# The last group of tails moved two to three turns earlier, and the first 22 tiles placed from six units' counts

## What is computed

```
h = concat(patches @ W + b with a class token and position embedding, txt)
h = h + attention(layernorm(h))                 # 12 heads of 16, rotary, causal
x = layernorm(h)                                # 8768 tokens, all samples together
pc = softmax(x @ Wsc + bsc); e = argmax(pc)     # "common" expert, 4 of them
dropped = rank of a token in its expert by -pmax >= capacity (2192)
u = argmax(softmax(x @ Wsu + bsu))              # "unique" expert, 4 of them
out = h + ffn_common[e](x) + dropped * ffn_unique[u](x)     # ffn: 192 -> 768 -> 192, gelu
```

## Time and profile before

| what | value |
|---|---|
| median of 3 runs | 1402.95 us (1399.99, 1402.95, 1414.35) |
| the profiled execution | 1410.49 us, its span 1408.7 us |
| mean granted TensorE clock in it | 0.941 |
| PE busy | 1227.0 us, 87% of the span |
| DVE, POOL, ACT busy | 905.9, 623.0, 557.8 us |
| data moved | 177.93 MB, mean 126 GB/s |

### The profile page before, as it was taken

How to read it: one execution, slowest core, us unless ns; L and a number is a source line. 1 busy time by engine, 2 the same in 40 slices (tenths; PEclk the granted TensorE clock), 3 DMA queues, 4 the chain that set the end, 5 groups by cost and what they waited for, 6 DMA issues and landing times.

```text
span 1408.7 us, 33272 instructions
## 1 busy us (share of the span) xinstructions
PE 1227.0 (87%) x12722; PEld 1041.6 (74%) x12722; DVE 905.9 (64%) x2063; ACT 557.8 (40%) x959; POOL 623.0 (44%) x990
## 2 busy tenths in 40 slices
PE   5889999999999999999999997648997778989983
PEld 4667777777777777777777766538896677989983
DVE  5676776786786786787787785467875333445431
ACT  1234334334334334334334343224453333545540
POOL 4133333334544444444444434426326364655654
PEclk9899999999999999999999997659998897999997
DMA  6001211212322322322322312477766364777740
GB/s 206 21 20 45 73 39 47 77 59 83 127 63 84 125 66 83 122 69 83 122 69 82 102 51 84 148 288 255 268 237 192 122 210 156 257 246 262 235 151 25
DMA packets 84368, 177.93 MB, mean 126 GB/s; under 512 B 16446, under 2 KB 57701, under 8 KB 84208
## 3 DMA queue, kind: packets, MB, share of 16 engines
q1 hardware_dynamic: 70544, 146.93, 32.2%
q0 software_dynamic: 13664, 28.84, 5.7%
HBM read 129.15 MB, written 50.38 MB: 127 GB/s over the span
## 4 chain that ended last, share of the span: by engine, by line
PE 43%; DVE 21%; issue 14%; POOL 10%; ACT 6%; another core or an unknown queue 2%; DMA 2%; SPq 1%; DVEq 0%; POOLq 0%; ACTq 0%
PE h_ps L1655 10%; PE y_ps L1666 10%; DVE capped L971 4%; ACT PT L739 3%; PE gen L502 3%; PE round_banks L582 3%; POOL sorted_d L226 3%; DVE xn L987 3%; POOL PT L853 3%; PE round_banks L555 2%; PE gen L544 2%; DVE nm L975 2%; PE gen L511 2%; DVE nm L973 2%
## 5 line engine op out<-in xcount | busy, mean ns | idle before, releaser
L739 ACT ACTIVATE PT<-round_banks 128x1752 f32<-128x1752 f32 x96 | 156.6, 1631 | 176.7 <-PE round_banks L582 176.7
L853 POOL TENSOR_SCALAR_AFFINE_SELECT PT<-PT 128x512 f32<-128x512 f32 x192 | 117.7, 637 | 212.5 <-ACT PT L739 212.0
L1745 ACT ACTIVATE Gl<-h_ps,W 128x256 f32<-128x256 f32 x264 | 117.3, 474 | 233.6 <-PE h_ps L1655 141.4
L1655 PE MATMUL h_ps<-XH,Wh 128*128 128x256 f32 x528 | 155.6, 310 | 51.2 <-issue 32.3
L1666 PE MATMUL y_ps<-W,Gl 128*128 128x192 f32 x1056 | 186.6, 331 | 0.9 <-issue 0.9
L1666 PEld LDWEIGHTS y_ps<-W,Gl 128*128 128x128 f32 x1056 | 176.5, 194 | 1.1 <-issue 1.1
L1655 PEld LDWEIGHTS h_ps<-XH,Wh 128*128 128x128 f32 x528 | 107.5, 204 | 57.7 <-issue 44.4
L502 PE MATMUL gen<-w_emb,xT 128*128 128x192 f32 (+1 forms) x768 | 142.5, 337 | 7.6 <-DMA ident<-in_ident_dram 7.6
L1655 PE MATMUL h_ps<-XH,Wl 128*128 128x256 f32 x528 | 145.5, 295 | 0.0
L1814 DVE TENSOR_TENSOR Wl<-W,Wh 128x768 fp32r<-128x768 f32 x88 | 84.2, 957 | 88.0 <-ACT Wh L1725 58.9
L1554 POOL DMA_INDIRECT out_dram<-Y,sid x76 | 81.3, 1070 | 134.3 <-DVE Y L1838 112.6
(11 more groups left out here) (273 smaller groups left out, 2467.0 us busy)
## 6 DMA issues: line engine op xcount, KB each, us to landing
W<-in_experts_dram SPq DMA_DIRECT2D x44, 771.0 KB
W<-in_experts_dram SPq DMA_DIRECT2D x44, 672.0 KB
xT<-in_xT_dram SPq DMA_DIRECT2D x32, 591.0 KB
X<-sorted_d SPq DMA_DIRECT2D x35, 450.0 KB
stage<-rows_d SPq DMA_DIRECT2D x64, 224.0 KB
rows_d<-xn SPq DMA_DIRECT2D x32, 256.0 KB
rows_d<-h SPq DMA_DIRECT2D x32, 192.0 KB
out_dram<-h SPq DMA_DIRECT2D x32, 192.0 KB
```

The lines of the kernel that those rows point to most:

```text
L739: act.activation(PT[(JG * b + j) % 2][:], R[:, :, 0:438], ACT.Exp, scale=SCALE).then_inc(exps, 1)
L853: pool.affine_select(x[:, :, at:at + P], x[:, :, at:at + P], [[0, GH], [1, P]], ALU.is_ge, 0.0, base=0, channel_multiplier=-1)
L1655: mm = pe.matmul(h_ps[f % 3][:, 0:ROWS], w[t.par][:, cols], x, start=(k == 0), stop=(k == len(products) - 1))
L1745: act.activation(Gl[t.par][:, f, :], h_ps[f % 3][:, 0:ROWS], ACT.Gelu, bias=W[t.i][:, B1O + f:B1O + f + 1]).then_inc(g_ready, 1)
```

## The change

In the last group (7) the tail steps of lags 8 to 12 move from turns 36, 37, 38, 39, 40 to turns 35, 36, 36, 37, 37 (`HURRIED`). The table `FINAL` says the order of banks in turns 35 and 36. On PE `rank` of unit 6 goes to the front of turn 36, the transposes `X2t` behind those of sample 31, `RTt` behind `RT`. On DVE `position` of unit 6 goes ahead of the copies of logits in turn 36, and `soften` waits for both copies. `early_tiles` goes from turn 37 to turn 33 and uses the counts of six units; EARLY is 22 in place of 26. The first row load waits for the scatters of units 0 to 5. `load_both` depends on EARLY, so it is issued at tiles 24 to 26 in place of 28 to 30.

```diff
--- before.py
+++ after.py
@@ -51,7 +51,7 @@
 RC = DX + D
 RW = RC + 2
 GROUP = 3
-EARLY = -(-(N - N // NG - NX * (ROWS - 1)) // ROWS)
+EARLY = -(-(N - 2 * (N // NG) - NX * (ROWS - 1)) // ROWS)
 NOWHERE = 2.0 ** 14
 AWAY = 2.0 ** 17
 KTH = CT
@@ -68,11 +68,19 @@
 TURNS = 4 * (NG - 1) + 12 + 1
 
 
+LAST = 4 * (NG - 1)
+HURRIED = {"8": LAST + 7, "9": LAST + 8, "10": LAST + 8, "11": LAST + 9, "12": LAST + 9}
+FINAL = {LAST + 7: [use for use in STEADY if use[0] not in ("ATt", "WO", "WOt")] + [("ATt", "8"), ("WO", 4), ("WOt", "8")],
+         LAST + 8: [("RK", "12"), ("X2", 5), ("X2t", "9"), ("RT", 5), ("RTt", "10")]}
+
+
 def item(lag, t):
 
     if isinstance(lag, str):
+        if HURRIED.get(lag) == t:
+            return NG - 1
         g, rest = divmod(t - int(lag), 4)
-        return g if rest == 0 and 0 <= g < NG else None
+        return g if rest == 0 and 0 <= g < NG - (lag in HURRIED) else None
     return t - lag if 0 <= t - lag < B else None
 
 
@@ -80,7 +88,7 @@
 
     table = {}
     for t in range(TURNS):
-        for use, lag in uses:
+        for use, lag in FINAL.get(t, uses) if uses is STEADY else uses:
             if item(lag, t) is not None:
                 table[use, item(lag, t)] = len(table)
     return table
@@ -96,6 +104,7 @@
     def __init__(self, t):
         self.t = t
         self.new, self.pre, self.mid, self.at, self.fin, self.end = (item(k, t) for k in range(6))
+        self.hurried = t >= LAST + 7
         self.tail = {k: item(str(k), t) for k in (0, 1, 7, 8, 9, 10, 11, 12)}
 
 
@@ -612,6 +621,8 @@
             for t in map(Turn, range(TURNS)):
                 if t.t == 2:
                     pe.wait_ge(later_in, 16 * len(later))
+                if t.hurried and t.tail[12] is not None:
+                    rank(t.tail[12])
                 if t.mid is not None:
                     for c in range(3):
                         have(f"KQ{c}", t.mid)
@@ -653,6 +664,9 @@
                 if t.end is not None:
                     pe.wait_ge(xn2_ready, t.end + 1)
                     turn_tokens("X2", t.end, xn2[t.end % 2], 2)
+                if t.hurried and t.tail[9] is not None:
+                    pe.wait_ge(xn2t_ready, t.tail[9] + 1)
+                    turn_tokens("X2t", t.tail[9], xn2t, 1)
                 if t.pre is not None:
                     project("V1", t.pre, xnT, w_qkv, 1, slice(2 * D, 3 * D))
                 if t.at is not None:
@@ -666,10 +680,10 @@
                         pe.wait_ge(consts_set, n_set)
                     pe.wait_ge(xnt_ready, t.tail[0] + 1)
                     turn_tokens("XTt", t.tail[0], xnt, 1)
-                if t.tail[8] is not None:
+                if t.tail[8] is not None and not t.hurried:
                     have("UTt", t.tail[8])
                     turn_tokens("ATt", t.tail[8], attt, 1)
-                if t.tail[10] is not None:
+                if t.tail[10] is not None and not t.hurried:
                     have("X2t", t.tail[10])
                     route("RTt", t.tail[10], x2tT, 1)
                 if t.tail[7] is not None:
@@ -684,12 +698,18 @@
                 if t.end is not None:
                     have("X2", t.end)
                     route("RT", t.end, x2T, 2)
-                if t.tail[12] is not None:
+                if t.hurried and t.tail[8] is not None:
+                    have("UTt", t.tail[8])
+                    turn_tokens("ATt", t.tail[8], attt, 1)
+                if t.hurried and t.tail[10] is not None:
+                    have("X2t", t.tail[10])
+                    route("RTt", t.tail[10], x2tT, 1)
+                if t.tail[12] is not None and not t.hurried:
                     rank(t.tail[12])
                 if t.tail[0] is not None:
                     have("XTt", t.tail[0])
                     project("QKt", t.tail[0], xntT, w_qkv, 0, slice(0, 2 * D))
-                if t.tail[9] is not None:
+                if t.tail[9] is not None and not t.hurried:
                     pe.wait_ge(xn2t_ready, t.tail[9] + 1)
                     turn_tokens("X2t", t.tail[9], xn2t, 1)
                 if t.pre is not None:
@@ -795,6 +815,9 @@
 
                         act.wait_ge(g_filled[bank("WO", t.fin - 1)], nth("WO", t.fin - 1))
                     copy_tokens("AT", t.fin, attT, 2)
+                if t.hurried and t.tail[8] is not None:
+                    act.wait_ge(g_filled[bank("WOt", t.tail[8] - 1)], nth("WOt", t.tail[8] - 1))
+                    copy_tokens("ATt", t.tail[8], atttT, 1)
                 if t.tail[9] is not None:
                     if t.tail[9]:
 
@@ -1190,6 +1213,8 @@
                     dve.wait_ge(r_emptied, 4 * b + 3)
                     dve.wait_ge(capped_read, JG * b + JG)
                     dve.tensor_tensor(x[:, :, 2], x[:, :, 1], x[:, :, 2], ALU.min).then_inc(nmax_ready, 1)
+                if t.hurried and t.tail[12] == NG - 2:
+                    position(t.tail[12])
                 if t.tail[10] is not None:
                     g = take("RTt", t.tail[10])
                     emptied("RTt", t.tail[10], dve.tensor_copy(by_token[:, UNIT * t.tail[10] + UNIT - 1, :], g[:, 0:NE]))
@@ -1204,14 +1229,16 @@
                     emptied("RT", t.end, dve.tensor_copy(by_token[:, c:c + 2, :].rearrange("p c e -> p (c e)"), g[:, 0:2 * NE]))
                 if t.tail[10] is not None:
                     dve.wait_ge(g_emptied[bank("RTt", t.tail[10])], nth("RTt", t.tail[10]))
+                    if t.hurried:
+                        dve.wait_ge(g_emptied[bank("RT", t.end)], nth("RT", t.end))
                     soften(t.tail[10])
                 if t.tail[11] is not None:
                     choose(t.tail[11])
-                if t.tail[12] is not None:
+                if t.tail[12] is not None and not (t.hurried and t.tail[12] == NG - 2):
                     position(t.tail[12])
                 if t.tail[12] == NG - 1:
                     pads()
-                if t.t == 4 * (NG - 2) + 13:
+                if t.t == 4 * (NG - 3) + 13:
                     early_tiles()
                 if t.tail[0] is not None:
                     g = t.tail[0]
@@ -1417,7 +1444,7 @@
 
                 if t.number == 0:
                     for half in range(2):
-                        sp.wait_ge(sorted_out[half], 16 * GROUP * len(range(half, GROUP * (NG - 1), 2)))
+                        sp.wait_ge(sorted_out[half], 16 * GROUP * len(range(half, GROUP * (NG - 2), 2)))
                 if t.number >= DEPTH:
                     sp.wait_ge(sid_ready, t.n - (DEPTH - 1))
                 row = sp.value_load(lrow[0:1, bass.ds(t.n, 1)], min_val=0, max_val=NX * RN - ROWS)
```

## The result

The changed kernel took 1389.23 us (median of 19 runs, 1373.77 to 1407.21), the kernel before beside it 1402.26 us (19 runs, 1390.1 to 1414.37). The ratio is 0.9892, with a 95% interval from 0.9864 to 0.992: 11 to 19 us less. The sum had said 6.6 us and 1396 us. The profiled execution of the changed kernel took 1401.2 us (span 1399.4), 12 us above its own median, where the one of before lay 8 above; so stretches are compared here, and spans only with care.

What follows compares the result with a forecast made beforehand. No engine was full where attention runs out (891 to 923 us); a chain of short steps bound it. Shorter chain 5.4 plus tile 0's idle 1.2 made 6.6 us: 1402.95 - 6.6 = 1396 us, range 1386 to 1407.

Steps and rivals of the forecast that it cites:

- Step A: PE, turn 35: tails' projection follows sample 31's, whose sum starts 0.5 us later; tails' sum `ht` done at 901.9.
- Step B: DVE, turn 36: waiting for `ht` makes sample 31's norm 2.0 us late; unit 6's `position` still ends 1.3 us early.
- Step C: Logits to `left`: tails' logits copied at 910.5 against 916.13, `early_tiles` out of the chain; DVE behind `left` at 917.6.
- Step D: SP's way to `left` through load 20: ends at 917.8, next limit by 0.1; both ways together gain 5.4 us.
- Step E: Opening of tile 0: rows wait only for units 0 to 5, so the idle before `XH` goes: 1.2 us.
- Steps at nothing: `early_tiles` in turn 33, POOL's masks beside it, tile 4's earlier weights and `load_both`'s new place: all counted as no gain.
- rival 1: Tiles 4 to 7: the sorting's head start removes SP's 5.8 us delay; 12.4 us gained, 1391; chance 0.16.
- the sum did not become 6.3: Turn 33: if DVE's steps and POOL's masks blocked each other, the total gain would be 6.3 us, not 6.6.
- the slack that the forecast had counted: Turn 33: POOL takes sample 29's statistics 2.0 us after their end, covering the 0.8 us that `early_tiles` delays.
- Rival 2: Tiles 24 to 26: late loads among list scatters bring more ACT waits, 25 - 6.6 us slower, 1421; chance 0.10.
- Rival 3: From 1064 us on: unnamed waits set by transfers swallow the gain, leaving 0 to 2 us, 1402; chance 0.16.
- Rival 4: SP's way to `left`: landing takes 2 us more behind twelve tail transfers; 4.6 us gained, 1398; chance 0.12.

Runs made afterwards that it cites:

- tails_only: Kernel before plus hurried tails alone, without early counts (26 early tiles, run right behind unit 6's position): 1396.56 against 1400.06 us, ratio 0.9986.
- changed_again: The changed kernel, unedited, timed again on a second chip beside the kernel before: 1327.22 against 1337.8 us, ratio 0.9926.
- weights_first: The changed kernel with SP's load 20 put behind tile 0's weights and rows, third chip: 1329.14 us, ratio 0.9941 to the kernel before.
- changed_third: The changed kernel, unedited, timed on a third chip beside the kernel before: 1328.8 against 1337.13 us, ratio 0.994.
- seven_units: The changed kernel, but tile 0's rows wait for seven units' scatters again, second chip: 1332.47 us, ratio 0.9964 to the kernel before.
- early_only: Kernel before plus the early part alone (22 early tiles from six units, early rows, late loads at tiles 24 to 26): 1398.38 us, ratio 0.9974.
- late_rows_moved: Kernel before with only the three late row loads moved from tiles 28 to 30 to 24 to 26, first chip: 1406.46 us, ratio 1.0054.
- late_rows_moved_2: Kernel before with only the three late row loads moved to tiles 24 to 26, repeated on the third chip: 1335.65 us, ratio 1.0.

## Why the prediction was right, and where its sizes were off

The time fell into the range, the sign and the mechanism were right, and the forecast of 6.6 us was too small: behind the sum of sample 31 the traces give 8.0 to 9.0 at the first up matmul and 9.0 to 9.5 at tile 11, and the timings 15, 9.9 and 8.0, each with 2.6 to 4 us to either side. The 1.08% of the first timing even falls into "faster by over 1%", to which the forecast gave 0.12; the 0.74 and 0.6% of the later ones do not. At the first up matmul the 7.8 us of the first two traces are 6.3 of earlier release (steps A to D, forecast 5.4), the 1.19 of idle (step E, as forecast) and 0.25 of tests that ran shorter (10.09 us from the release to `Wl`, now 9.84).

- **Step A** put `ht` at 901.9; it was at 900.96 on DVE. In the other traces of this front `ht` is 0.46 to 1.28 us behind `h`, never the 1.7 of the forecast.
- **Step B** said the norm would be 2.0 late; it was at 903.38 in place of 904.45. `position` of unit 6 ended at 907.2, forecast 908.7.
- **Step C**: logits copied at 909.15, forecast 910.5; DVE's first step behind `left` at 916.80, forecast 917.6. The rest of the chain had the length taken for it. But `early_tiles` was not the larger part: tails_only, which keeps it ahead of this copy, had the copy 10.97 us behind the sum of sample 31, where before it was 16.44 and in changed_again 9.46. So 5.5 us came from the tails' earlier turns and 1.5 from `early_tiles`: only a part of its 3.57, since without it DVE waits 1.93 us for PE there. In turn 33 it was free for the rest of the chain, as said.
- **Step D**: SP's load 20 ended at 916.54, forecast 917.8, and was the last, by 0.37 us, forecast 0.1. The cover that the prediction named as next is the one that is there: weights_first took it away, and the idle at `left` went with it. But that load is not free to move, for behind it tile 1's weights left 3.5 us later against changed_third.
- **Step E** is right as a remainder and mis-sized in what it stands for. It added 1.2 us, the idle of the earlier trace rows, as if the early rows only cured that. Yet with `left` 6.3 us earlier and the first scatter of unit 6's last load only 3.7 us earlier (920.25 against 923.93), the rows' wait would have grown, to 3.0 us in seven_units; the early wait is worth 3.1 us at the first up matmul and 4.0 by tile 3. Its second weights and the transfers of tiles 1 to 3 stand behind tile 0's rows in SP's queue (tile 0's second weights left at 922.85 in seven_units and at 916.45 in changed_again); that these make the last us is argued, not shown. The shorter chain alone brings 4.8 (tails_only), not 5.4; the early part alone 2.1 (early_only). Together they bring 8.0 to 9.0, more than the 6.9 of the two, because each removes what would have held the other.
- **Steps at nothing**: `load_both`'s place is worth nothing on the third chip (1.0, within 0.23%). Tile 4's weights left 10.2 us earlier, and no tile was shorter for it: 70.8 us from tile 3 to tile 11, as before. So **rival 1**, which added 5.8 us for that, is refuted, though a time near its 1391 was measured. Beside `early_tiles` POOL's first masks took 1.22 us as without it, so the sum did not become 6.3. The Trainium skill (SBUF — State Buffer, Who interferes with whom) has a VectorE step with two SBUF inputs and a GpSimd step that reads SBUF block each other, for the whole step of whoever is first. The trace fits it on DVE's side, in one step: `used` took 0.53 us where POOL's mask had begun 0.11 ahead of it, and 0.15 in changed_again, where the mask began 0.03 behind it (871.50 and 871.47). It cost 0.38 us of the slack that the forecast had counted, and the chain nothing.
- **Rival 2** (slower by the late rows among the scatters) needs ACT's pauses to come from that pile-up. On two chips the same scatters ran without one pause. It is refuted there; late_rows_moved on the first chip (slower by 0.15 to 0.93%) is not explained by it, since the changed kernel has the same loads there. **Rival 3** (given back from 1064 on) is refuted for all but 1.3 to 1.4 of 9.0 us: the rest of the gain is there at tile 30. **Rival 4** had SP 2 us late; it was early against the forecast.

What stays open: whether the 11 to 19 us of the first timing hold some us beyond the 9 of the front. The medians there are 13.0 us apart, with 19 runs each that spread over 24 and 33 us. ACT's pauses differ by 25 us in the two traces (65.2 and 40.2), yet from tile 11 to tile 30 both take the same time (211.9 and 211.6), and no run took the pauses away on the same chip.

## What to carry to other kernels

When a change moves two things that end in the same place, price each with the other already done: a wait of 1.2 us that looks like a remainder grows as the neighbouring chain gets shorter. Measure from an event just ahead of the change (here the sum of sample 31), not from the start of the span: the three traces of the unchanged kernel's front lie within 0.2 us of each other that way (37.5 to 37.7) and those of the changed one within 1.0 (28.75 to 29.7), where twelve timed runs on the first chip could not tell 4.8 us from none. A pause without a releaser should not be given a cause by what runs beside it before it was seen on a second chip.

## What the runs showed of the hardware

The kernel before took 1400 us on one chip and 1337 us on two others. The first 780 us have the same busy time of PE (723.82 us in before, 723.43 in changed_again) and the same granted clock of 0.98. The difference lies in the tiles: in the four traces of the first chip and the two of the first timing ACT waits 39.6 to 65.2 us for a releaser without a name, in 15 to 19 pieces, inside tiles, while PE too is idle for nothing that the trace names; on the others there is not one. From tile 11's result to tile 30's it is 212 us in before (1065.30 to 1277.20) and 154 in late_rows_moved_2 (1055.71 to 1209.60), the same code but for the place of three loads. In one such pause of the kernel before, on PE and ACT in the middle of a tile's up matmuls:

```profile
1080.86 0.48 PE L1655 MATMUL h_ps<-XH,Wh 128*128 128x256 f32 x1 [3.90 <-issue]
```

```profile
1080.24 0.47 ACT L1745 ACTIVATE Gl<-h_ps,W 128x256 f32<-128x256 f32 x1 [9.64 <-remote]
1084.47 0.47 ACT L1745 ACTIVATE Gl<-h_ps,W 128x256 f32<-128x256 f32 x1 [3.76 <-remote]
```

This pause cost more than its length. PE stood still from about 1077 to 1081, and from 1081 to 1088 the granted clock was 0.50, the lower of its two levels (1.2 GHz), where it had been 1.00 (2.4 GHz) up to 1077; the same matmul took 0.41 us in place of 0.28.

One reading of engines that stop inside a tile, with no releaser that the trace names, is that their instructions come late. The Trainium skill (Runtime: NRT & Kernel Launch, Instruction fetch mechanics) calls the cost of going from one block of code to the next "mostly hidden". The second and third chip agree, with no such pause, and the traces of the first speak against the reading too. The queues that fetch instructions moved the same 104 and 56 packets in all fourteen runs, with 0.5 and 0.1% of the time, and from 1069 to 1088 us, across the pauses above, the kernel before has no packet of theirs on record. What makes the pauses stays open.
